# A fused patch embedding, top-k attention and mixture-of-experts kernel: GpSimd forms differences to the threshold, an exclusive or folds the two sides into one list, three batches share an embedding

## What is computed

```python
h = _layernorm(concatenate([cls, patches @ W + b]) + pos) * gamma + beta
h = concatenate([h, txt])
scores = einsum('bhid,bhjd->bhij', q, k) * scale      # q, k, v of layernorm(h)
topk_scores, indices = top_k(scores, int(T * 0.3))    # 49 of 165
attn = softmax(masked)                                # all others -inf
h = h + (attn @ v) @ W_out.T + b_out
h = h + moe(layernorm(h)) + shared(layernorm(h))
```

## Time and profile before

| | |
|---|---|
| median of 3 runs | 3370.57 us (3353.76 to 3374.98) |
| the profiled execution | 3362.61 us |
| its span | 3360.9 us |
| first and last `flag` (L1130) | 128.3 and 2941.2 us |
| TensorE, VectorE, ScalarE, GpSimd busy, share of the span | 82%, 84%, 83%, 64% |
| instructions | 82985 |

### The profile page before, as it was taken

How to read it: one execution, slowest core, us unless ns; L and a number is a source line. 1 busy time by engine, 2 the same in 40 slices (tenths; PEclk the granted TensorE clock), 3 DMA queues, 4 the chain that set the end, 5 groups by cost and what they waited for, 6 DMA issues and landing times.

```text
span 3360.9 us, 82985 instructions
## 1 busy us (share of the span) xinstructions
PE 2740.0 (82%) x22281; PEld 2098.7 (62%) x22281; DVE 2809.3 (84%) x11013; ACT 2785.1 (83%) x12673; POOL 2167.3 (64%) x3409
## 2 busy tenths in 40 slices
PE   4688888888888888888888888988888888647776
PEld 3466666666666666666666666666666666436665
DVE  1899999999999999999999999999999999822222
ACT  3999999999999999999999999999999999611111
POOL 3456767667676667767766676776676766444554
PEclk7899999999999998999999999999999999868888
DMA  1001100000000000000000000000000000016776
GB/s 51 11 14 20 20 21 21 21 21 20 14 20 20 21 21 21 21 15 19 20 20 21 21 21 21 18 17 20 20 21 21 21 20 17 11 38 158 174 176 139
DMA packets 181453, 116.34 MB, mean 35 GB/s; under 512 B 100208, under 2 KB 172484, under 8 KB 180964
## 3 DMA queue, kind: packets, MB, share of 16 engines
q1 hardware_dynamic: 146596, 91.60, 10.0%
q0 software_dynamic: 34368, 19.34, 3.9%
HBM read 66.51 MB, written 33.40 MB: 30 GB/s over the span
## 4 chain that ended last, share of the span: by engine, by line
DVE 38%; ACT 27%; PE 13%; issue 12%; DMA 4%; POOL 3%; DVEq 1%; SPq 1%; POOLq 0%; ACTq 0%
ACT JK L831 14%; DVE PR L1175 6%; DVE S L1028 5%; DVE ML L1070 5%; DVE MU L1047 4%; ACT E L819 4%; DVE XU L1037 4%; ACT SIDE L850 4%; DMA E<-x_rows,ids_t 2%; DMA out<-E,ids_t 2%; PE bank L1521 2%; DVE XL L1057 2%; PE bank L1676 1%; DVE RD L1180 1%; ACT PTT L861 1%
## 5 line engine op out<-in xcount | busy, mean ns | idle before, releaser
L831 ACT ACTIVATE JK<-S,thr 128x165 f32<-128x165 f32 x2688 | 1124.0, 442 | 3.4 <-POOL thr L562 1.7
L607 POOL DMA_INDIRECT slot_token<-TOKI,SLOT x512 | 541.3, 1057 | 202.8 <-issue 182.6
L850 ACT ACTIVATE SIDE<-S,t 128x165 f32<-128x165 f32 x1344 | 572.4, 447 | 9.4 <-POOL t L574 4.4
L831 ACT ACTIVATION_READ_ACCUMULATOR JK<-S,thr 128x1 f32 x2688 | 565.0, 210 | 0.0
L819 ACT ACTIVATE E<-bank,nb 128x165 f32<-128x165 f32 x1344 | 523.8, 418 | 14.6 <-DVE S L1028 14.4
L1175 DVE SCALAR_TENSOR_TENSOR PR<-S,TV,E 128x165 f32<-128x165 f32 x1344 | 434.1, 379 | 0.0
L1028 DVE TENSOR_SCALAR_CACHE_REDUCE S<-bank 128x165 f32<-128x165 f32 x1344 | 357.9, 314 | 12.5 <-PE bank L1504 10.5
L1047 DVE MAX8 MU<-XU 128x8 f32<-128x165 f32 x1344 | 349.2, 311 | 0.2 <-DVE XU L1037 0.2
L1070 DVE MAX8 ML<-XL 128x8 f32<-128x165 f32 x1344 | 339.7, 307 | 0.7 <-POOL XL L589 0.7
L1037 DVE SCALAR_TENSOR_TENSOR XU<-SIDE,S 128x495 f32<-128x495 f32 x448 | 317.0, 708 | 11.9 <-ACT SIDE L850 11.4
L589 POOL TENSOR_TENSOR XL<-SIDE,S 128x495 f32<-128x495 f32 x256 | 308.0, 1203 | 28.9 <-ACT SIDE L850 14.3
(11 more groups left out here) (196 smaller groups left out, 6981.8 us busy)
## 6 DMA issues: line engine op xcount, KB each, us to landing
S<-in_w_gate SPq DMA_DIRECT2D x64, 192.0 KB, 2.7
S<-in_w_up SPq DMA_DIRECT2D x64, 192.0 KB, 3.3
S<-in_w_down SPq DMA_DIRECT2D x64, 192.0 KB, 3.4
x_rows<-X SPq DMA_DIRECT2D x64, 160.0 KB
H<-in_txt SPq DMA_DIRECT2D x64, 128.0 KB, 5.9
QA<-QT SPq DMA_DIRECT2D x512, 10.3 KB
QB<-QT SPq DMA_DIRECT2D x512, 10.3 KB
out<-OT SPq DMA_DIRECT2D x64, 128.0 KB
```

Of the source, the lines that this page charges most:

```text
L607: pool.indirect_dma_start(slot_token, bass.IndirectOffsetOnAxis(SLOT[r % 2][:, 0, k:k + 1], 0), TOKI[r % 2][:, :], None, bounds_check=SLOT ...
L831: act.activation(JK[:, t % 4, :], S[r % 2][:, t, :], ACT.Sign, bias=(t0, t1)[n][:, t:t + 1], scale=-1.0, accum_out=(c0, c1)[n][:, t:t + 1] ...
L850: act.activation(SIDE[:, t % GROUP + GROUP * (g % 2), :], S[r % 2][:, t, :], ACT.Sign, bias=t2[r % 2][:, t:t + 1], scale=-1.0, accum_out=c ...
```

## The change

- Differences on GpSimd (`apart`): X = (S - t2) x 2^-40 for each tile, 21 tensor_scalar instructions a batch, into five buffers of three tiles. `under` and `above` are gone, on both engines, and so are SIDE, XU and XL.
- The third count reads X. ScalarE makes it for groups 0 to 2 (`third_count`, Sign), VectorE for groups 3 to 6 (`third_count`, X < 0, with a sum).
- `side` and `side2` turn the counts into a word of bits for each row (`flip`), and `one_side` applies an exclusive or to the group as int32, in place. It leaves on top the values of the side on which the 49th lies, the nearest largest. One MAX8 for each tile (`nearest`) fills LIST; the second MAX8 is gone.
- Rank, candidates and threshold work on one list of 8 values a row, and the threshold is formed back by an exclusive or and t2. New checks; at most 6 values too many or 7 too few may lie below t2 (before at most 7 too many).
- The embedding is made for three batches at once (`TRIO` = 111 rows); the image rows go to HP and from there to H by a DMA (`load_image`).
- `general` loops over 21 tiles and, inside, over 6 rounds, in place of 7 groups of three tiles written out.
- The calls in `iteration` are put in another order on every engine.

```diff
-                dve.scalar_tensor_tensor(XU[g % 2][:, :, :], SIDE[:, at:at + GROUP, :], BIG, S[r % 2][:, GROUP * g:GROUP * (g + 1), :],
-                                         ALU.mult, ALU.min).then_inc(s_xu, 1)
...
-                    dve.max(MU[:, t, :], XU[g % 2][:, t % GROUP, :]).then_inc(s_mu, 1)
...
-                    dve.max(ML[:, t, :], XL[g % 3][:, t % GROUP, :]).then_inc(s_ml, 1)
...
-            def under(i, r, g):
...
+            def apart(i, r, g):
+
+                n = NG * i + g
+                pool.wait_ge(s_up, UP * i + (17 if g < AHEAD // GROUP else 20))
+                if n >= DEEP:
+                    pool.wait_ge(s_list, GROUP * (n - DEEP + 1))
+                for t in range(GROUP * g, GROUP * (g + 1)):
+                    last = pool.tensor_scalar(X[n % DEEP][:, t % GROUP, :], S[r % 2][:, t, :], t2[r % 2][:, t:t + 1], DOWN,
+                                              ALU.subtract, ALU.mult)
+                last.then_inc(s_xp, 1)
...
+                    act.activation(JL[:, n % 3, :], X[(NG * i + g) % DEEP][:, k, :], ACT.Sign, bias=tiny[:, :], scale=-1.0,
+                                   accum_out=c2[:, t:t + 1]).then_inc(s_c2, 1)
...
+                    dve.tensor_scalar(JD[:, n % 3, :], X[(NG * i + g) % DEEP][:, k, :], 0.0, None, ALU.is_lt, ALU.add,
+                                      accum_out=c2[:, t:t + 1]).then_inc(s_cd, 1)
...
+                dve.tensor_scalar(off[:, lo:hi], c2[:, lo:hi], scale, base, ALU.mult, ALU.add).then_inc(s_turn, 1)
...
+                dve.tensor_scalar(flip[:, lo:hi], off[:, lo:hi], FLIP, -FLIP, ALU.min, ALU.max).then_inc(s_turn, 1)
...
+            def one_side(i, g):
+
+                n = NG * i + g
+                dve.wait_ge(s_turn, TN * i + 2 * [g in v for v in SETS].index(True) + 2)
+                at = flip[:, GROUP * g:GROUP * g + GROUP].rearrange("p (n a) -> p n a", a=1).to_broadcast([P, GROUP, T])
+                bits = X[n % DEEP][:, :, :].bitcast(i32)
+                dve.tensor_tensor(bits, bits, at.bitcast(i32), ALU.bitwise_xor).then_inc(s_x, 1)
...
+                    dve.max(LIST[:, 0, WIN * t:WIN * t + WIN], X[n % DEEP][:, t % GROUP, :]).then_inc(s_list, 1)
...
+                with dve.If(dve.snap(unsure) > 0):
+                    with dve.Fori(0, NT) as t:
...
+                        with dve.Fori(0, ROUNDS):
+                            dve.sem_clear(s_slow)
+                            dve.max(W8[:, :], W).then_inc(s_slow, 1)
+                            dve.wait_ge(s_slow, 1)
+                            dve.match_replace(W, W8[:, :], W, LOW).then_inc(s_slow, 1)
+                            dve.wait_ge(s_slow, 2)
```

More of the change, by code:

```diff
@@ L289, in parcels, with share, trio, of_trio @@
             return 16 * sum(m > 0 or at == PACKED - 1 for m in range(n % 2, n + 1, 2))
+        def share(i, groups, g):
+            return len(groups) * i + sum(k < g for k in groups)
+        TRIOS = (n_batch + PACKED - 1) // PACKED
+        def trio(m):
+            return m % PACKED == 0 and 0 <= m // PACKED < TRIOS
+        def of_trio(n):
+            return [b for b in range(PACKED * n - PACKED + 1, PACKED * n + 1) if b >= 0]
         def known(i):
@@ L391, in iteration @@
                     diagonal(i + 1, 1)
+                if has(i + 2) and not (known(i) and i == -1):
+                    load_text(i + 2, (r + 2) % RING)
                 if has(i - 3):
                     store_out(i - 3, (r - 3) % RING)
+                if has(i + 2):
+                    load_image(i + 2, (r + 2) % RING)
+                if trio(i + 7):
+                    load_patches((i + 7) // PACKED)
+                if has(i - 3):
                     store_x(i - 3, (r - 3) % RING)
[L395 to L396 removed]
+                    pack(i - 3, (r - 3) % RING)
             def load_expert(e, k):
@@ L681, in iteration @@
-                if has(i):
-                    refine(i, r, 1)
-                if has(i - 4):
-                    back_slots(i - 4, r, 6, 8)
+                if trio(i + 4):
+                    front_affine((i + 4) // PACKED)
                 if has(i):
@@ new lines, in side2, with sides @@
+            def side2(i, k):
+                lo, hi = span(k)
+                dve.wait_ge(s_turn, TN * i + 2 * k + 1)
+                if k == 0:
+                    ahead(dve, s_sel, SEL * (i - 1) + 4, i - 1)
+                dve.tensor_scalar(flip[:, lo:hi], off[:, lo:hi], FLIP, -FLIP, ALU.min, ALU.max).then_inc(s_turn, 1)
+            def sides(i):
+                dve.wait_ge(s_turn, TN * i + 2 * len(SETS))
+                ahead(dve, s_sel, SEL * (i - 1) + 7, i - 1)
+                dve.tensor_scalar(turn[:, :], off[:, :], 1.0, -1.0, ALU.min, ALU.max).then_inc(s_turn, 1)
@@ L1322, in iteration @@
                 if has(i - 1):
-                    uppers(i - 1, 2)
+                    third_count(i - 1, 3)
+                    side(i - 1, 0)
+                    side2(i - 1, 0)
+                if has(i + 1):
+                    front_norm2(i + 1, (r + 1) % RING)
+                if has(i - 1):
+                    one_side(i - 1, 0)
+                if has(i - 3):
+                    back_glu(i - 3)
+                if has(i - 1):
+                    one_side(i - 1, 1)
+                    one_side(i - 1, 2)
                 if has(i - 3):
@@ L1342, in iteration @@
                 if has(i - 1):
-                    uppers(i - 1, 3)
+                    side2(i - 1, 1)
+                if has(i):
+                    take(i, r, 5)
+                if has(i - 1):
+                    third_count(i - 1, 6)
+                    one_side(i - 1, 3)
                 if has(i - 3):
@@ L1346, in iteration @@
                 if has(i - 1):
-                    above(i - 1, (r - 1) % RING, 5)
+                    side(i - 1, 2)
+                    nearest(i - 1, 3)
+                if has(i):
+                    take(i, r, 6)
+                if has(i - 1):
+                    side2(i - 1, 2)
+                    one_side(i - 1, 4)
                 if has(i - 3):
                     back_top3(i - 3)
-                if has(i):
-                    take(i, r, 5)
-                    take(i, r, 6)
+                if has(i - 1):
+                    sides(i - 1)
+                    one_side(i - 1, 5)
                 if has(i - 3):
```

775 lines of the change are left out of this document (393 added, 382 removed).

## The result

The changed kernel takes 3653.99 us (median of four, 3647.07 to 3660.69) beside 3371.27 us: 1.085 times as long, 95% interval 1.0803 to 1.0896. The forecast was 3190 us. The general path was not entered.

A forecast was written before the change was run, and what follows sets the result against it. VectorE and ScalarE were taken as full at 42.25 of 44.65 us, GpSimd third at 38.0. Rings of 41.1, 40.8 and 38.5 us plus 0.7 gave 41.8 us, -180 us over 63 periods: 3190 us, 8-in-10 range 3100 to 3310.

The forecast's parts named there:

- GpSimd's price: Each of 21 new differences a batch on GpSimd was priced like `KZ`, 0.485 us, 10.2 us in all.
- the text's own rule: GpSimd's time per batch is 30.6 + 21p us, p being the price of one difference.
- rival 3: GpSimd becomes the outright bound, its differences ahead of everything ScalarE waits for; 46.5 us a period, 3487 us; chance 0.07.
- ScalarE: 37.2 forecast: ScalarE loses twelve sign counts a batch, 5.0 us, and falls from 42.25 to 37.2 us a period.
- VectorE's busy time: VectorE loses 14.2 us and gains 10.7 us of work a batch, from 42.25 to 38.7 us.
- The exclusive or's duration: VectorE's int32 exclusive or over 495 elements was expected to show a duration of 0.65 us, like `XU`.
- The gap at the branch: VectorE's gap at the branch over the general path at each batch's end: 1.5 us taken, bounds 0.65 and 1.65.
- The wait before `off`: VectorE waits 0.9 us in every batch for ScalarE's nine counts before it can form `side`.
- VectorE's ring: VectorE's work, branch gap and new wait per batch: 38.7 + 1.5 + 0.9 = 41.1 us, between 39.5 and 43.
- The 38.0 us: GpSimd's occupied time per period before the change, taken as 44.65 us less 6.6 us of waits.
- SLOT: SLOT now comes just ahead of the masks, with eight mask tiles behind it to cover TensorE's 2.3 us of sums.
- Rival 5: The general path is entered for a batch, costing 140 to 210 us; one such batch eats the gain; chance 0.04.

The follow-up runs named there:

- f1_add: The changed kernel with GpSimd's differences written as an addition of the negated threshold instead of a subtract; 3152.04 us, ratio 0.9361.
- e4_body: The kernel before with only the general path's shorter body, two nested loops; 3375.79 us, ratio 0.9958.
- The dose runs: f1_add with 3 or 9 of the 21 differences put back in the subtract form; 3461.95 and 3606.92 us.
- e2_add: The same program as f1_add, the changed kernel with differences as an addition, in an earlier job; 3452.42 us, ratio 1.0189.
- e10_both: f1_add's program with `front_v` moved behind the transposes on TensorE and `back_scale` behind the last `refine2` on GpSimd; 3487.78 us, ratio 1.0275.
- f4_both: The same program as e10_both, run again in another job; 3278.50 us, ratio 0.9728.
- e1_forms: The kernel before with eleven instruction forms on GpSimd and two on VectorE, four of each, added to the setup; 3423.64 us, run once.
- f3_after: The changed kernel again, without an edit, in the same job as f1_add; 3645.74 us, ratio 1.0822.
- g3_add: f1_add again, without an edit, as the anchor of the dose runs; 3424.63 us, ratio 1.0082.

## Why the prediction was wrong

**The step that failed** is GpSimd's price: "`KZ` is the same form: 485 ns on the page's mean". It has the same shape and number of steps, but `KZ` adds and the difference subtracts. I bounded the price by `KZ`'s own minimum and maximum, 0.445 and 0.758 us, so the range was a range of contention and not of the operation, and 0.935 lay outside it. No row of the trace before has a tensor_scalar subtract on GpSimd (only VectorE's, in `XN` and `TK`), and that was the sign to see. It is seen in the kernel's lines alone, since the profile calls an add and a subtract both TENSOR_SCALAR. A price that no row shows needs ends further apart, the more as it is taken 21 times a batch. By the text's own rule, 30.6 + 21 x 0.935 = 50.2 us against 49.2 measured: the mechanism of rival 3 was right, with 0.07 of chance. Its cause was not: neither of its reasons for or against (a lock between VectorE's and GpSimd's long operations) made the 850 ns, which stand with VectorE idle. Contention, a lock or another, can have made at most the difference between the median 850 and the mean 935.

**The rest of the sum held, in part by errors that cancel.** With the cheap form, and without TensorE's condition, the whole change is worth what was forecast and a little more: 3152 us against 3190, period 41.3 us against 41.8. That is the test of the other terms, since f1_add has all of the change but the subtract.

- ScalarE: 37.2 forecast, 37.4 in f1_add, 38.0 in the changed kernel.
- VectorE's busy time: 38.7 forecast; 38.6 and 37.9. The exclusive or's duration is 660 ns at the median, as was asked of it; `JD` is 320 ns, as the takes are.
- The gap at the branch: I took 1.5 us of 0.65 to 1.65. In f1_add VectorE's first take of a batch stands 1.26 us behind the last work ahead of the branch (57 batches, 0.81 to 2.14). The waits view gives this gap the names of GpSimd's and TensorE's last work, and how much of it is the branch is not shown. The 0.76 us of e4_body are from a job in which this gap is shorter in the kernel before too.
- The wait before `off`: 0.9 us forecast, in f1_add 16.5 us over 63 batches, 0.26.
- VectorE's ring is then 37.9 + 1.26 + 0.26 = 39.4 us and not 41.1. What the ring lacked are short waits for TensorE: 47.8 us for scores, 21.6 for the sum ahead of the flag and 14.9 for the context up to the last flag, 1.4 us in each of 59 periods. With them VectorE comes to 40.8 of 41.3 us. So the forecast period came near by terms that were 1.7 us too dear and 1.4 us left out: the size was luck in part. The low end of its bounds, 39.5, does not add up either: 38.7 - 1.4 + 0.65 + 0.9 = 38.9.
- GpSimd at the price 0.424 (f1_add's mean): 30.6 + 8.9 = 39.5 us of 41.3, so it is nearly level, as forecast. The dose runs, though under TensorE's condition, fit some slack and not much. That is also why 9.3 to 10.7 us more on GpSimd (21 x 0.443 by medians, 21 x 0.511 by means) came out as 7.9 us of period. The recorded text says that descriptor work is shown as "issue" and not as busy; the trace before shows both, 512 indirect DMAs of `back_slots` at a mean of 1057 ns busy and 182.6 us of "issue" ahead of them. The 38.0 us are untouched, since they were taken from the waits.
- SLOT: "eight mask tiles behind it to cover" it was right where TensorE gets its instructions (VectorE waits 14.9 us for the context in f1_add up to the last flag, 59 periods) and wrong where it doesn't (247.7 us in 57 periods of e2_add). The old order suffers from the same condition far less, since its context stands in a longer wait for SLOT and VectorE has other work behind it; that it costs the kernel before 20 to 25 us (3391 against 3367) and this order 209 (e10_both against f4_both, one chip) to 300 (e2_add against f1_add, two chips) is measured, the reason for the difference is argued.
- Rival 5 did not occur.

**What stays open.** What starves TensorE's burst in some jobs. The instruction queues move the same 165 and 284 packets in e2_add and f1_add; it was there in jobs on three chips, and on one of the three it was missing in an earlier and a later job, with identical programs. I did not find a way to set it. That it is instruction fetch is not shown: the view says only that TensorE waited for nothing it can name. But the traces show that the burst stops at a count and not at a time. In e2_add the first `<-issue` gap stands behind 42 to 48 matmuls of the burst in 50 of 57 bursts, 2.0 to 5.3 us after its start; in e4_body it stands behind exactly 66 in 35 of 58; in f1_add none of 60 bursts has one. That is what a supply of instructions that runs out would look like. How long TensorE waits ahead of the burst does not decide it: in e4_body that is 109.4 us in 58 times, 1.89 us, with the condition, and in the kernel before 107.1 in 58, 1.85, without it. The condition is more than this one row, since VectorE's gap at the branch is shorter where it holds: 0.92 us in e1_forms, 1.65 in the earlier trace rows, with the same body. The changed kernel itself, unmoved, was never measured under this condition.

## What to carry to other kernels

A row prices an instruction only for the same engine and the same operation: before one form is put 21 times a batch on an engine with 4 us to spare, look for its very operation in the kernel's lines, and where there is none, run the form by itself, as e1_forms does, before the price is used. No undisturbed row would have bounded it here: `H<-TK,BET` with two inputs takes 0.72 us for 256 elements, which by my estimate is 0.47 for 165, and the form took 0.85. In a tensor_scalar on GpSimd in 32-bit floats write a - b as a + (-b), with the sign taken where it is cheap: in one job this turned an 8.2% loss (f3_after) into a 6.4% gain (f1_add); in two other jobs, with TensorE's condition, the add form was still 1.9% and 0.8% slower than the kernel before. Compare rows, too, only inside one job: the gap of e4_body looked halved beside a trace from another. And repeat a kernel side by side before believing in a gain that three unlike edits all bring.

## What the runs showed that I had not expected

- GpSimd's tensor_scalar with subtract and mult: 864 ns at 128x165 and 1962 at 128x495, with add and mult 402 and 688; on VectorE 298 and 300.
- One program, e2_add, took 3452 us in one job, 3152 in another and 3425 in a third. In the slow ones TensorE has `<-issue` waits at its burst, 119.4 and 109.5 us in 2600 us. In the burst shown, matmuls started every 35 ns run dry after 1.6 us, and the clock is then granted at 0.50 for some us. The Trainium skill (Runtime: NRT & Kernel Launch, Instruction fetch mechanics) says that fetching is hidden because instructions are dispatched more slowly than they arrive; f1_add agrees with it, e2_add, if it is the fetch that stalls, does not.
- Among kernels that differ by one move in an order, such a condition can turn the sign: f1_add is 6.4% faster than the kernel before, g3_add, the same program, 0.8% slower (1.0082).
